# A two-layer decoder on one core: attention 1 and cross attention reordered (last value quarter, turned queries and keys, two weight merges, outer units)

## The reference

```
x = x + attention(layernorm(x))      # layer 0: decaying linear attention; layer 1: softmax, 16 heads of 16, rotary, causal
x = x + cross(layernorm(x), ctx)     # layer 0: sigmoid link matrix; layer 1: 16 heads, low-rank queries and keys
x = x + experts(layernorm(x))        # router, top 6 of 16 experts, plus a shared expert
```

```
q = x @ wq.T ; k = x @ wk.T ; v = x @ wv.T      # heads of 16
q, k = rotate(q), rotate(k)                     # x*cos + swapped(x)*sin
s = where(causal, q @ k.T / 4, -inf) ; out = softmax(s) @ v @ wo.T
```

```
q_big = rotate((x @ Wq.T) @ w_kc_q)             # 192 wide
kv_r  = rotate(ctx)                             # 64 wide
s     = (q_big @ W_qr) @ (kv_r @ W_kr).T
out  += softmax(s) @ kv_r @ w_kc_kv.T @ Wo.T
```

## Time and profile before

| | |
|---|---|
| median of 3 runs | 962.04 us (956.76, 962.04, 969.21) |
| profiled execution: its own time | 964.97 us |
| its span | 963.2 us |
| mean granted PE clock | 0.984 of full |
| PE, DVE, ACT, POOL busy | 918.1, 613.7, 428.1, 101.2 us |
| start of attention 1's steps; of the merges; of unit 0; of experts 1's first gate | 358.3; 458.0; 489.5; 741.4 us |

### The profile page before, as it was taken

How to read it: one execution, slowest core, us unless ns; L and a number is a source line. 1 busy time by engine, 2 the same in 40 slices (tenths; PEclk the granted TensorE clock), 3 DMA queues, 4 the chain that set the end, 5 groups by cost and what they waited for, 6 DMA issues and landing times.

```text
span 963.2 us, 14200 instructions
## 1 busy us (share of the span) xinstructions
PE 918.1 (95%) x5380; PEld 706.2 (73%) x5380; DVE 613.7 (64%) x1176; ACT 428.1 (44%) x1069; POOL 101.2 (11%) x127
## 2 busy tenths in 40 slices
PE   7999789999999998999989999999999999999997
PEld 5666567888888786666767777777766778888886
DVE  2446775666666655666578687777776666666664
ACT  4533444333333438875344344443445543333342
POOL 2100100000000031000312232222220000000000
PEclk9799899999999999999999999999999999999999
DMA  5002101111110050000620000000001011111001
GB/s 165 1 1 85 50 17 43 56 47 38 46 33 1 1 218 1 1 1 1 251 85 1 1 1 1 1 1 1 1 1 50 18 50 50 50 49 49 16 0 45
DMA packets 12249, 36.80 MB, mean 38 GB/s; under 512 B 1920, under 2 KB 4192, under 8 KB 11424
## 3 DMA queue, kind: packets, MB, share of 16 engines
q1 hardware_dynamic: 12160, 36.02, 11.2%
q0 software_dynamic: 32, 0.01, 0.0%
HBM read 34.98 MB, written 1.05 MB: 37 GB/s over the span
## 4 chain that ended last, share of the span: by engine, by line
PE 88%; ACT 6%; DVE 4%; issue 1%; DMA 0%; POOL 0%; SPq 0%; ACTq 0%; DVEq 0%
PE ps L1222 80%; PE ps L1780 3%; PE ps L1380 2%; ACT Q L1023 1%; ACT whi L1038 1%; PE ps L1233 0%; DVE probs_q L777 0%; ACT probs_q L1129 0%; PE ps L1659 0%; DMA xb_w<-in_xb_w 0%; DVE stats L430 0%; DVE rope_buf L731 0%; DVE neg_max L767 0%; ACT silu_g L1063 0%; PE ps L1554 0%
## 5 line engine op out<-in xcount | busy, mean ns | idle before, releaser
L1068 ACT ACTIVATE h_hi<-weighted_h 128x512 fp32r<-128x512 f32 x100 | 63.2, 632 | 153.6 <-DVE weighted_h L609 153.5
L1222 PE MATMUL ps<-xT_first,whi 128*128 128x512 f32 x400 | 119.4, 400 | 1.2 <-ACT silu_g L1063 1.2
L1222 PE MATMUL ps<-xT_second,whi 128*128 128x512 f32 x400 | 116.0, 391 | 1.7 <-ACT silu_g L1063 1.7
L619 DVE TENSOR_TENSOR h_lo<-weighted_h,h_hi 128x512 fp32r<-128x512 f32 x100 | 69.2, 692 | 65.1 <-ACT h_hi L1068 64.9
L646 DVE TENSOR_TENSOR shared_gate<-silu_g,row_shares 128x512 f32<-128x512 f32 x88 | 60.9, 692 | 65.1 <-ACT silu_g L1063 65.0
L1063 ACT ACTIVATE silu_g<-ps 128x512 f32<-128x512 f32 x100 | 59.5, 596 | 77.1 <-PE ps L1222 77.0
L1222 PE MATMUL ps<-xT,merged_q 128*128 128x256 f32 x384 | 92.1, 383 | 0.0
L1222 PEld LDWEIGHTS ps<-xT_first,whi 128*128 128x128 f32 x400 | 75.2, 189 | 19.9 <-issue 2.6
L1222 PEld LDWEIGHTS ps<-xT_second,whi 128*128 128x128 f32 x400 | 74.3, 188 | 18.9 <-issue 3.5
L1214 POOL TENSOR_TENSOR latent_rot<-rope_buf 128x256 f32<-128x256 f32 x96 | 68.4, 733 | 186.4 <-DVE rope_buf L732 186.4
L1222 PE MATMUL ps<-h_hi,whi 128*128 128x512 f32 x200 | 79.6, 398 | 2.8 <-DVE h_lo L619 2.8
(11 more groups left out here) (182 smaller groups left out, 1565.4 us busy)
## 6 DMA issues: line engine op xcount, KB each, us to landing
raw<-in_ffn SPq DMA_DIRECT2D x50, 384.0 KB, 3.1
wx<-in_wx SPq DMA_DIRECT2D x4, 2048.0 KB, 9.5
cx<-in_cx SPq DMA_DIRECT2D x1, 1536.0 KB, 6.9
X<-in_x SPq DMA_DIRECT2D x4, 256.0 KB, 5.1
kvc<-in_kvc SPq DMA_DIRECT2D x1, 1024.0 KB, 14.3
out<-X SPq DMA_DIRECT2D x4, 256.0 KB, 2.2
wqkv<-in_wqkv SPq DMA_DIRECT2D x1, 768.0 KB, 6.9
wqkv<-in_wqkv SPq DMA_DIRECT2D x1, 512.0 KB, 6.2
```

The lines of the kernel that those rows point to most:

```text
L619: v.tensor_tensor(h_lo[:, u % 2, :], weighted_h[:, u % 2, :], h_hi[:, u % 2, :].bitcast(F32), ALU.subtract).then_inc(act_lo[l], 1)
L1068: a.activation(h_hi[:, u % 2, :], weighted_h[:, u % 2, :], ACT.Copy).then_inc(act_hi[l], 1)
L1222: return pe.matmul(o, l, r, start=start, stop=stop, skip_group_check=True)
```

## The change

In attention 1: value quarter 3 and the reciprocals of batch b move from the last step of the odd turn to the second step of the next even turn, the output product from that turn's third step to the first step of the odd turn; ACT's copy to og now stands at the second step. Batches 2 and 3 are turned at n = 4 and n = 7 into banks 0 and 1, with the queries copied by ACT (`turned_queries`) and the keys by DVE (`turned_keys`) after the maxima and copies of steps 5 and 7. The drain is written out anew, with the keys and outputs of merge 0 in it. In cross: merges 0 and 2 take keys and outputs ahead of queries; the wx loads wait for PE's products instead of ACT's copy; the context is transposed through bank 3; latent tile (1, 2) stands ahead of scores(0, 1), and tile (2, 0) ahead of query_side(1); output(13) stands ahead of the scores of unit 15; and the tail is put in another order on PE, ACT and DVE. The core of the diff:

```diff
-        RECIPROCAL_BANK = 1
+        def reciprocal_bank(b):
+            return 2 if b == NB - 1 else 1
+        def turn_bank(b):
+            return 0 if b >= 2 else 2
+        KV_TOKEN_BANK = 3
...
@@ sync
-                        sp.wait_ge(merged_o_copied, hg - 1)
+                        sp.wait_ge(pe_merged_q, 4 * (hg - 1))
+                        sp.wait_ge(pe_merged_o, hg - 1)
...
@@ vector, attention1 (steps; row_max and copy_transposed as before)
+                    if n == 5:
+                        turned_keys(NB - 2)
+                    if n == 7:
+                        turned_keys(NB - 1)
+                    if b >= 0 and (turn % 2, k) == (0, 0):
+                        reciprocals(b)
+                    if b >= 0 and (turn % 2, k) == (0, 2):
+                        if b >= 1:
+                            scaled(1, b - 1)
+                        spread_reciprocals(b)
+                    if b >= 1 and (turn % 2, k) == (1, 1):
+                        add_out(1, b - 1)
+                        norm_statistics(4, b - 1)
+                copy_transposed(STEPS - 2)
+                copy_transposed(STEPS - 1)
+                reciprocals(NB - 1)
+                scaled(1, NB - 2)
+                spread_reciprocals(NB - 1)
+                normalise(4, 0)
+                normalise(4, 1)
+                add_out(1, NB - 2)
+                scaled(1, NB - 1)
...
+            def turned_keys(b):
+                v.wait_ge(pe_turn, 2 * b + 2)
+                for half, sign in ((kE, "even_s"), (kO, "odd_s")):
+                    v.tensor_scalar(half[:, b].rearrange("p m s -> p (m s)"), ps[:, turn_bank(b) + 1, :], k(sign), None, ALU.mult).then_inc(k_turned, 1)
...
@@ vector, cross, unit w
                     if more:
                         rope(w + 1, 1)
+                    else:
+                        split_lo(1, 1, 1)
                     if w >= 1:
                         copy_transposed(w - 1, 1)
+                    if w == 0:
+                        rope(1, 2)
                     row_max(w, 1)
                     normalise_probs(w, 0)
-                    if more:
+                    if more and w >= 1:
                         rope(w + 1, 2)
...
@@ scalar, attention1, step n
+                    if n >= 2:
+                        copy_transposed(n - 2)
+                    if b >= 1 and (turn % 2, k) == (0, 1):
+                        copy_mixed(b - 1)
+                    probabilities(n)
+                    if n == 5:
+                        turned_queries(NB - 2)
+                    if n == 7:
+                        turned_queries(NB - 1)
...
@@ tensor, attention1, step n (b = turn // 2 - 1)
+                    scores_by_query(n)
+                    if n < 2:
+                        query_or_key(NB - 1, n)
+                    if n >= 2:
+                        transposed_probabilities(n - 2)
+                    if n == 4:
+                        turned(NB - 2)
+                    if n == 7:
+                        turned(NB - 1)
+                    if b >= 1 and (turn % 2, k) == (0, 1):
+                        mixed_probabilities(b - 1, 3)
+                        reciprocals_by_feature(b - 1)
+                    if b >= 0 and (turn % 2, k) == (0, 2):
+                        if b == 0:
+                            pe.wait_ge(q_ready, 2 * NB)
+                        mixed_probabilities(b, 0)
+                    if b >= 0 and (turn % 2, k) == (1, 0):
+                        mixed_probabilities(b, 1)
+                        if b >= 1:
+                            output(1, b - 1)
+                    if b >= 0 and (turn % 2, k) == (1, 1):
+                        mixed_probabilities(b, 2)
+                transposed_probabilities(STEPS - 2)
+                transposed_probabilities(STEPS - 1)
+                mixed_probabilities(NB - 2, 3)
+                reciprocals_by_feature(NB - 2)
+                pe.wait_ge(wx_in[0], 16)
+                merged_keys(0)
+                for quarter in range(4):
+                    mixed_probabilities(NB - 1, quarter)
+                reciprocals_by_feature(NB - 1)
+                output(1, NB - 2)
+                merged_outputs(0)
+                output(1, NB - 1)
...
@@ tensor, cross, merge hg
+                    if hg == 2:
+                        merged_keys(hg)
+                        merged_outputs(hg)
+                    merged_queries(hg)
+                    if hg % 2:
+                        merged_keys(hg)
+                        merged_outputs(hg)
...
@@ tensor, cross, unit w
+                    if w == 1:
+                        latent_queries(2, 0)
                     query_side(w)
-                    if more:
+                    if more and w != 1:
                         latent_queries(w + 1, 0)
+                    if not more:
+                        output(w - 2)
                     scores(w, 0)
...
+                    if w == 0:
+                        latent_queries(1, 2)
                     scores(w, 1)
-                    if more:
+                    if more and w >= 1:
                         latent_queries(w + 1, 2)
-                    if w >= 2:
+                    if w >= 2 and more:
                         output(w - 2)
...
+                tokens_turned(1, 0)
                 output(UNITS - 2)
                 transposed_probabilities(UNITS - 1, 0)
+                router_logits(1, 0)
                 transposed_probabilities(UNITS - 1, 1)
-                tokens_turned(1, 0)
+                logits_by_token(1, 0)
                 weighted_contexts(UNITS - 1)
-                router_logits(1, 0)
+                gate_half(1, 0, 0, False, 0)
                 output(UNITS - 1)
-                gate_half(1, 0, 0, False, 0)
-                logits_by_token(1, 0)
                 up_half(1, 0, 0, False, 0)
```

More of the change, by code:

```diff
@@ L574, in attention1 @@
                         project1(b, j)
[L575 to L588, removed]
-                            scaled(1, b - 1)
[L590 to L597, removed]
+                for n in range(STEPS):
+                    turn, k = divmod(n, 3)
+                    b = turn // 2 - 1
+                    row_max(n)
+                    if n < 2:
+                        project1(NB - 1, n)
+                    if n >= 2:
[8 more added lines that the diff above has]
+                        if b >= 1:
+                            scaled(1, b - 1)
+                        spread_reciprocals(b)
+                    if b >= 1 and (turn % 2, k) == (1, 1):
+                        add_out(1, b - 1)
+                        norm_statistics(4, b - 1)
@@ L983, in attention1 @@
                         turned(b - 1)
[L984 to L1001, removed]
@@ L1002, in attention1 @@
-                norm(4, NB - 1)
+                for n in range(STEPS):
+                    turn, k = divmod(n, 3)
+                    b = turn // 2 - 1
+                    if n >= 2:
+                        copy_transposed(n - 2)
+                    if b >= 1 and (turn % 2, k) == (0, 1):
[5 more added lines that the diff above has]
+                        turned_queries(NB - 1)
@@ L1004, in turned @@
             def turned(b):
-                a.wait_ge(pe_turn, 2 * b + 1)
-                a.activation(qT[:, b].rearrange("p m s -> p (m s)"), ps[:, 2, :], ACT.Copy).then_inc(q_ready, 1)
+                turned_queries(b)
                 a.wait_ge(pe_turn, 2 * b + 2)
@@ L1662, in y_tokens, with part_of, merged_queries, merged_keys @@
                         last.then_inc(pe_y_tokens, 1)
+            def part_of(slot, name, rows=P):
+                a, b = XP[name]
+                return wx[0:rows, slot, a:b]
+            def merged_queries(hg):
+                wq = part_of(hg % 2, "wq").rearrange("p (h d) -> p h d", h=4)
+                kcq = part_of(hg % 2, "kcq").rearrange("p (h q) -> p h q", h=4)
+                for jj in range(4):
+                    if hg >= 1:
+                        pe.wait_ge(merged_q_copied, 4 * (hg - 1) + jj + 1)
+                    if hg == 2 and jj < 2:
+                        pe.wait_ge(rope_products, 6 - 2 * jj)
+                    for kk in range(KD):
+                        last = mm(ps[:, jj, XQ * kk:XQ * kk + XQ], wq[:, jj, 128 * kk:128 * kk + 128], kcq[:, jj, :], True, True)
+                    last.then_inc(pe_merged_q, 1)
+            def merged_keys(hg):
+                qrT = part_of(hg % 2, "qrT", XR).rearrange("p (h f) -> p h f", h=2)
+                krT = part_of(hg % 2, "krT", XR)
+                for part in range(2):
+                    if hg >= 1:
+                        pe.wait_ge(merged_s_copied, 12 * (hg - 1) + 6 * part + 6)
+                    for j in range(3):
+                        last = mm(ps[:, 4 + part, 128 * j:128 * j + 128], qrT[:, part, 128 * j:128 * j + 128], krT[:, XC * j:XC * j + 2 * XC], True, True)
+                    last.then_inc(pe_merged_s, 1)
+            def merged_outputs(hg):
```

(10 more changed lines are left out.)

150 lines of the change are left out of this document (65 added, 85 removed).

## The result

The changed kernel takes 949.51 us (median of 4 executions, 948.84 to 950.79) against 962.48 (4 executions, 956.76 to 969.21): a ratio of 0.9867, 95% interval 0.9824 to 0.9911, 13.0 us faster. The profiled execution took 948.84 us with a span of 947.0.

The account below looks back on a forecast made before the run. PE, busy 918.1 of 963.2 us, was taken as the bound, with 17.8 us of waits within reach. Seven gains summed to 12.3 us: 964.97 became 952.7, carried to the median 949.7, stated as 951, range 943 to 960.

Parts of the forecast that it names:

- Start of attention 1: Turning batches 2 and 3 later cuts PE's waits there from 4.9 to 1.6 us: gain 3.3.
- Later halves: Moving the last value quarter and reciprocals fills the waits on the eight exponentials in even halves: gain 2.1 us.
- Hand-over and merges: Hand-over to cross, waits from 2.4 to 1.8 us, gain 0.6; merges, waits on rotation products and xT go, gain 2.1.
- Units 0 and 1: In cross, moved latent tiles fill waits on exponentials and latent_rot, but unit 1 takes 1.4 on tSl: gain 1.1 us.
- Last unit and tail: At the end of cross, reordered outputs, tokens and logits cut waits from 3.3 to 1.8 us: gain 1.5.
- Clock: Three slices of attention 1 lost 3.1 us to a lower granted clock; half comes back with less idling: gain 1.6.
- Rival 1: ScalarE sets the pace of attention 1, so the gain is only 6.8 us, time 955; chance 0.13.
- rival 4: The gaps move one step on instead of closing; gain 0 to 4 us, time 958 to 962; chance 0.11.
- rival 3: The low clock settles in attention 1 or cross; one stretch losing 7 us leaves 958; chance 0.07.
- the mark of 28 us: Span at the 1.2 GHz level from which the low clock decides against the change; 32 us gives 964 to 966.
- Rival 2: The weights of the merges in cross arrive late, so time is 953 to 954; chance 0.09.

Follow-up runs that it names:

- e8: Changed kernel with every merge in the old order (queries, keys, outputs) and merge 0 whole behind the last output product; median 953.15 us.
- e10: Changed kernel with latent tile (2, 0) back behind query_side(1) and batch 2's last value quarter between the transposes of steps 21 and 22; median 947.31 us.
- e9: Kernel before with only the late turns: batches 2 and 3 turned at steps 4 and 7 through banks 0 and 1, keys by VectorE; median 956.88 us.
- e1: The kernel before, run again with nothing edited; median 962.90 us.
- e3: Changed kernel with the last value quarter and reciprocals of batches 0 and 1 back at the last step of their half; median 951.24 us.
- e5: Changed kernel with latent tile (2, 0) back behind query_side(1), tile (1, 2) staying ahead of scores(0, 1); median 945.43 us.
- e11: Changed kernel with output(13) behind the scores of unit 15 and the tail of cross in the old order; median 950.47 us.
- e2: Changed kernel with batches 2 and 3 turned at steps 1 and 3 again through banks 2 and 3, copied by ScalarE; median 956.44 us.
- e7: Changed kernel with tile (2, 0) behind query_side(1), batch 2's last quarter between transposes of steps 21 and 22, and scaled(3) ahead of add_out(2); median 946.73 us.

## Why the prediction was right

It said 951, 943 to 960, within 2% of before; measured were 949.51 and a ratio of 0.9867. Its own sum gave 949.7. The mechanism was right: PE's waits fell by 11.0 us where 10.7 were forecast, and every sign that it named for being right came (no wait above 0.7 us at steps 2 to 8, the 1.17 waits gone, 1.26 before step 22, none on rope_buf, 1.41 on tSl in unit 1 and none in unit 15, the clock at 1.00 through attention 1). That sum and time agree to 0.2 us is luck: the parts below miss by up to 0.9 in both directions, and the median depends on the clock of attention 0. That the changed kernel's four times lie within 2.0 us is luck too; other kernels with the late turns spread by 9 to 13 us (e8, e10, e9).

The starts of the same instructions in e1 and the changed kernel split the 11.7 us without a rest: 4.2 from step 0 to step 9, 2.3 to the transposes of step 21, 2.8 to unit 0, 1.4 to unit 2, 0.0 to unit 15 and 1.0 to the end. Step by step:

- **Start of attention 1:** 3.3 forecast, 4.2 measured (4.1 in e9). The scores of step 8 waited 0.31 and the first values 0.32, where I had 0.6 and 0.65, and 0.17 where I had 0.35 in small waits. ScalarE had more lead than I gave it.
- **Later halves:** 2.1 forecast, 2.3 measured (2.3 in e3 too); both waits went entirely.
- **Hand-over and merges:** 0.6 and 2.1 forecast, 2.8 for the two together. By waits it is 2.4 to 2.1 in the hand-over, a gain of only 0.3, and 2.4 to 0.25 in the merges, 2.1; the rest, some 0.4, is open. The waits named stand in the profile after: 1.26 for "about 1.0", 0.44 for 0.5, 0.43 for 0.3, 0.25 for 0.3. e8's 2.7 is the price of another edit (the merges' order with the new drain kept) and equals this by chance. The 0.9 us on xT went with bank 3, which no run tests alone.
- **Units 0 and 1:** 1.1 forecast, 1.4 measured. The query side of unit 2 begins 15.18 us earlier (516.43 to 501.25) where unit 0's began 13.80 earlier (489.48 to 475.68). The exchange of latent_rot for 1.4 us on tSl came as said; e5 shows that it was needless.
- **Last unit and tail:** 1.5 forecast, 1.0 measured (0.9 in e11). Mis-sized: output(14) still waited 0.41 where I had nothing, and of the 1.57 us by which the first up product came earlier relative to unit 15 (742.96 to 726.15, less 15.24), 0.6 was lost again by the end, 0.28 of it on h_lo, where I had 0.4.
- **Clock:** 1.6 forecast. From step 0 on the first profile is 2.8 us longer than e1 by its drops, and e1 had none: against e1 the change could win nothing by the clock. The term exists only on average. The drops of the earlier trace rows were also read short: the window from 405 to 410 us, not listed there, has 0.94, another 0.3 us. Of the three profiles with early turns two fell in attention 1, of the ten with late turns none. That speaks for a part of the term being the change's own, but three profiles don't show it, and the drop of 0.72 followed a wait of 1.17 us, not the longest. Over all executions with a clock on record, the one of 1513.02 us left out, (1 - mean granted clock) x time is 14.4 us in the 68 with early turns and 12.6 in the 55 with late ones, a difference of 1.8 with about 1.5 either way, which neither confirms nor refutes 1.6.

Rival 1 is refuted by 0.5 us of waits on Q; rival 4 by 6.8 us of waits in the two stretches where 14 were its mark; rival 3 did not occur in the changed kernel but did in e2. Its prices rest on two bases: 958 keeps the old drops of the clock, the mark of 28 us takes them away, so by the first base a stretch of 32 us would give 967, not 964 to 966. Rival 2 was near: PE's weight load waited 0.3 us for wx in merge 2, though PE itself did not stand still for it.

## What to carry to other kernels

When one engine is full, list its waits, and for each ask which independent work already in its order could stand there; but check what that work covered where it stood (moving the quarter in the drain uncovered a wait of 1.26 us, moving tile (2, 0) one of 1.41 on tSl). Before trusting differences of a few microseconds, measure from the point where the edit begins: here an unedited stage scattered by 12.6 us, as much as the whole change gives. Or compare executions of the same mean granted clock. And the longest wait is the first to look at: besides its own time, two of three profiles lost a stretch at the low clock behind it.

## What the runs showed of the hardware

The granted clock after one and the same wait differs by execution. Behind the 1.9 us wait at step 4 it stayed at 1.00 (e1), gave 0.87 and 0.79 in two windows (the kernel before), or fell to 0.50 for over 10 us with PE busy throughout (e2). The kernel before has a second drop, to 0.72, behind a wait of 1.17 us at step 14; e3 and e9 have waits of that length at the same place and stayed at 1.00. In the ten profiles of kernels with late turns, the changed one and e3 to e11, no window of 5 us in attention 1's steps was below 1.00. What decides between these outcomes was not tried.

At equal mean clock the same kernel repeats closely (e7: 946.13, 946.43 and 947.03 us at 0.987), and with it moves by microseconds: 941.86 at 0.994, 954.86 at 0.978.
